# One eigensolver on one Trainium2 core: a factor formed on other engines, levels interleaved, fewer waits inside an engine

## The chip, the core and the metric

The program runs on one core of a Trainium2 chip. Its time is the time of one execution on the device in microseconds (us), given as the median of several runs. Engines are named as in the profile: PE is TensorE, DVE is VectorE, ACT is ScalarE, POOL is GpSimd, SP is SyncE. Everything is float32.

## The reference, cut to what matters

Input `x` is (128 batches, 128 nodes, 128 features) and `adj` is a 128x128 symmetric matrix. Two layers follow each other:

```
deg = sum(A, 0) + sum(A, 1) - diag(A)
L   = rsqrt(deg)[:, None] * (diag(deg) - A) * rsqrt(deg)[None, :]
_, U = eigh(L)                                   # 128 eigenvectors
h = relu(layernorm(x))
x = x + einsum('nm,bmd->bnd', U, relu(einsum('mn,bnd->bmd', U.T, h) @ W1 + b1) @ W2 + b2)
h = relu(layernorm(x))
x = x + conv_and_LSTM(h)        # two graph convolutions, then windows of 1 to 4 nodes through LSTM cells
```

The signs of the eigenvectors must be those that the reference's solver gives, because a ReLU stands between `U.T` and `U`.

## The kernel before, in words

The first half of the time is the eigensolver, and it is a serial chain. Engines run their own instruction streams and wait for each other on semaphores. Nothing is scheduled automatically: the order in each stream is the order in which the code stands. In order of time DVE does this:

1. **Householder**, 127 steps that make the matrix tridiagonal (DVE, PE and ACT in turn). After 16 steps POOL gets a 16x16 corner and starts 16 sweeps of its own (the `leaf` tiles, `Fori` at L307): they settle the sign of the leaf and end with `leaf_sign` (L378).
2. **Statistics and the orthogonal factor** (L906 to L956). Layer norm statistics of `x`, then `QT` from the Householder vectors: six rounds in which DVE copies two PE results out of PSUM and PE multiplies them again, and two more products. DVE waits for PE in each.
3. **First Sturm count** (`sturm`, L974 to L999): 127 steps on 128x16 tiles from both ends of the matrix, then one comparison over 128x2048 and one sum over it. Then 16 comparisons, each multiplied with ones by PE and summed in PSUM (L1004, L584). **Second Sturm count** likewise, without the products.
4. **Setting up four levels** (L1019 to L1033): `D4`, `EV`, `lam4` and `wrow` hold the matrix cut in 1, 2, 4 and 8 blocks.
5. **Two twisted passes** (`twisted`, L1039 to L1088): 127 recurrence steps of 8 lanes, then for each of the four levels, one after the other, a chain of 128x128 instructions that ends in a vector `V4[:, l]`.
6. **Tail** (L1092 to L1158): normalizing, the deflation and sign rules, `QT` times the vectors, two refinements in which DVE and PE alternate, the last signs, and `eig_done`.

In DVE's stream two helpers do the waiting. `op` (L742) waits for the instruction that it has just issued before the next one may start. `ask` (L746) issues one, tells PE, and then waits for PE's answer. POOL has an `op` of the same kind (L311), so each of its 88 instructions in a sweep waits for the one before.

While DVE runs the second Sturm count and the first twisted pass, PE and ACT transpose and multiply the normalized `x` for the first layer (`turn`, `first_product`). PE's stream is in order: the `QT` products, the transposes of the LSTM weights (L570 to L581), the 16 count products (L584), then this work. After `eig_done` the first layer's products start (L629), then the LSTM rounds follow; nothing of that part depends on how the eigensolver was done.

Of the kernel before, what the change touches and what calls it, by code (L numbers as in the profile page):

```python
# [11 lines left out]
F = 16  # L12
# [47 lines left out]
def build(nc, t_in, out):  # L60
    with ExitStack() as ctx:
# [21 lines left out]
        scp = sb("scp", [N, 64])  # L83
# [98 lines left out]
        stv = sem("stv")  # L182
        stored = sem("stored")
# [40 lines left out]
        ring = [spare[:, (8 + c) * GW:(9 + c) * GW] for c in range(RING)]  # L224

# [46 lines left out]
        def _(pool):  # L272
# [34 lines left out]
            with nc.gpsimd.Fori(0, QR_SWEEPS) as k:  # L307
# [20 lines left out]
                for c, v in enumerate((d16[:, 1:16], d16[:, 0:15], e16[:, 0:15])):  # L328
                    op(TT(pick[:, c, 0:15], v, oh[:, 0:15], ALU.mult))
# [29 lines left out]
                for w in (1, 2, 4, 8):  # L359
                    op(TT(lift[:, w:LEAF], now[:, w:LEAF], y16[:, 0:LEAF - w], ALU.mult))  # L360
# [23 lines left out]
        def _(act):  # L384
# [17 lines left out]
            nc.scalar.activation(ln[:, 2, :], ln[:, 1, :], ACT.Sqrt).then_inc(ln_dev, 1)  # L402
            for c in range(2 * SKIPS):
                act.wait_ge(w_turned, c + 1)
                nc.scalar.activation(wT[:, c // SKIPS, c % SKIPS, :], banks[c % 2][:], ACT.Copy).then_inc(w_kept, 1)
# [114 lines left out]
        def _(pe):  # L520
# [34 lines left out]
            mms((B[3], M[1]), (B[4], Um))  # L555
            mms((B[3], M[1], M[0]), (B[4], M[0], M[1]))
            for r in range(6):
                if r < 5:
                    mms((B[5], M[4], M[6]), (B[3], M[4], M[3]), (B[4], M[3], M[4]))
                else:  # L560
                    mms((B[5], M[4], M[6]))
            mms((B[3], M[7], M[8]))
            mms((B[3], M[8], M[5]))
# [18 lines left out]
            for f in range(F):  # L582
                pe.wait_ge(stv, f + 1)
                ins = nc.tensor.matmul(banks[6][:, 0:1], BIG[:, f * N:(f + 1) * N], ones[:, 0:1],  # L584
                                       start=(f == 0), stop=(f == F - 1))
# [28 lines left out]
            mms((B[3], V4[:, 0, :]), (banks[6][:, 0:1], sc[:, 30:31].to_broadcast([N, N]), ones[:, 0:1]))  # L614
            mms((B[3], M[1], QT[:]), (B[4], QT[:], M[1]), (banks[5][:, 0:1], QT[:], sc[:, 31:32]))
            for r in range(REFINES):
                mms((B[3], Lap[:], U[:]))
                mms((B[4], U[:], M[0]), (B[5], U[:], U[:]))
                mms((B[6], ones[:], M[5]))
                mms((B[3], UT[:], M[5]), (B[4], M[5], UT[:]))  # L620
            mms((banks[3][:, 0:1], U[:], sc[:, 32:33]))
            mms((B[4], UT[:]))

            pe.wait_ge(eig_done, 1)
            for it in range(ROUNDS):
# [6 lines left out]
                for i in range(STREAMS):  # L632
# [6 lines left out]
                    last.then_inc(out_ready[i], 1)  # L639
                for i in range(STREAMS):  # L640
                    pe.wait_ge(out_kept[i], it + 1)
                    nc.tensor.matmul(bank[i][(3 * it + 2) % 2], UT[:], z0S[i], start=True, stop=True).then_inc(back_ready[i], 1)
# [94 lines left out]
        def _(dve):  # L737
# [27 lines left out]
            op(V.memset(UC[:], 0.0))  # L765
            dve.wait_ge(adj_in, 16)
# [139 lines left out]
            op(V.tensor_scalar(hB[:], hB[:], -1.0, None, ALU.mult))  # L906
# [30 lines left out]
            ask(V.tensor_tensor(M[2], A[:], I, ALU.mult))  # L937
            op(V.tensor_copy(dB[:], B[3]))
            op(V.tensor_tensor(M[1], B[4], below[:, 0:N], ALU.mult))
            ask(V.tensor_tensor(M[1], M[1], hB[:], ALU.mult))  # L940
            op(V.tensor_copy(M[0], B[3]))
            op(V.tensor_copy(M[8], B[4]))
            dve.wait_ge(ln_var, 1)
            dve.wait_ge(ln_dev, 1)
            V.tensor_tensor(M[6], I, M[0], ALU.add).then_inc(to_pe, 1)
            inverse(slice(0, BATCH))
            answered[0] += 1
            asked[0] += 1
            dve.wait_ge(from_pe, answered[0])
            for r in range(6):  # L950
# [8 lines left out]
            LO, HI, H1, H2, LAM = 18, 19, 33, 34, 35  # L959
            op(V.scalar_tensor_tensor(out=M[0], in0=eB[:], scalar=-1.0, in1=eB[:], op0=ALU.mult, op1=ALU.max))  # L960
            op(V.tensor_copy(M[1], M[0]))
            op(V.tensor_tensor(M[1][:, 1:N], M[1][:, 1:N], M[0][:, 0:N - 1], ALU.add))
            op(V.tensor_tensor(M[3], dB[:], M[1], ALU.subtract))
            op(V.tensor_reduce(S(LO), M[3], AX_X, ALU.min))
            op(V.tensor_tensor(M[3], dB[:], M[1], ALU.add))
            op(V.tensor_reduce(S(HI), M[3], AX_X, ALU.max))
            op(V.tensor_scalar(S(H1), S(HI), S(LO), 1.001 / (N * F), ALU.subtract, ALU.mult))
            op(V.scalar_tensor_tensor(out=S(LO), in0=S(H1), scalar=-0.5, in1=S(LO), op0=ALU.mult, op1=ALU.add))
            op(V.tensor_tensor(M[2], eB[:], eB[:], ALU.mult))
            op(V.tensor_scalar(M[2], M[2], TINY, -1.0, ALU.max, ALU.mult))  # L970
# [3 lines left out]
            def sturm(sem):  # L974
# [43 lines left out]
            for l in range(LEVELS):  # L1018
                op(V.tensor_copy(D4[:, l, :], dB[:] if l == 0 else D4[:, l - 1, :]))  # L1019
                op(V.tensor_copy(EV[:, l, :], eB[:] if l == 0 else EV[:, l - 1, :]))  # L1020
                op(V.tensor_copy(lam4[:, l:l + 1], S(LAM)))
                for c in (SPLITS[l - 1] if l else []):
                    op(V.tensor_scalar(D4[:, l, c - 1:c + 1], D4[:, l, c - 1:c + 1], M[0][:, c - 1:c], None,
                                       ALU.subtract))
                    op(V.memset(EV[:, l, c - 1:c], 0.0))
            op(V.memset(wrow[:], 0.0))
            for l in range(3):
                for c in SPLITS[l]:

                    op(V.memset(wrow[:, l, c - 1:c], 1.0))  # L1030
# [64 lines left out]
            for l in range(LEVELS):  # L1095
                op(V.tensor_scalar(V4[:, l, :], V4[:, l, :], S(24 + l), None, ALU.mult))
# [202 lines left out]
```

## Time and profile before

| | us |
|---|---|
| median of 3 runs | 1615.69 (1614.9 to 1615.76) |
| the profiled execution, its own time | 1614.43 |
| its span in the trace | 1612.7 |
| DVE busy | 1164.6 (72%) |
| PE busy | 1207.6 (75%) |
| POOL busy | 508.7 (32%), all before 700 us but for one instruction |

The profile shares the chain of work that ended last as PE 55%, DVE 39%, issue 3%, ACT 3%. The span of the trace and the time of the execution differ by 1.73 us, which lie around the program. A busy share is an average over two halves: in the first DVE carries the chain, in the second PE. Starts in the timeline rows are counted from the start of the span, and two rows of one engine overlap where the second did not wait for the first.

### The profile page before, as it was taken

How to read it: one execution, taken by the hardware profiler on the slowest of the kernel's cores; microseconds unless marked ns; L12 is line 12 of the kernel's file. 1: busy time of each engine (PE TensorE's matmuls, PEld its weight loads, DVE VectorE, ACT ScalarE, POOL GpSimd, SP SyncE). 2: the span in 40 equal slices, each digit the busy share in tenths (PEclk: the TensorE clock that was granted, in tenths of full speed). 3: DMA queues.
4: the chain of work that ended last, by engine and by line, in shares of the span. 5: the costliest groups of instructions: out<-in, count | busy, mean ns of one | idle time of the engine just before them, and what ended most of it. 6: DMA issues, size and time to landing. Idle time of an engine off the chain costs nothing.

```text
span 1612.7 us, 26217 instructions
## 1 busy us (share of the span) xinstructions
PE 1207.6 (75%) x7124; PEld 1077.3 (67%) x7124; DVE 1164.6 (72%) x6182; ACT 790.9 (49%) x2549; POOL 508.7 (32%) x1426
## 2 busy tenths in 40 slices
PE   5666777775436500016989999999999999999998
PEld 4555666665335400005868989989898998989897
DVE  8999999998689999975775654645555564555545
ACT  1222222221219700001237868688786868868676
POOL 0277777777887778720000000000000000000000
PEclk9999999999859955556999999999999999999999
DMA  9200000000000000000310000000000000000000
GB/s 269 58 1 1 1 1 1 1 1 1 1 0 1 1 0 0 1 1 26 101 32 1 2 26 0 26 0 13 13 0 26 0 26 0 0 26 0 26 1 27
DMA packets 43626, 28.77 MB, mean 18 GB/s; under 512 B 1520, under 2 KB 39440, under 8 KB 43536
## 3 DMA queue, kind: packets, MB, share of 16 engines
q1 hardware_dynamic: 43536, 27.81, 6.1%
q8 instruction: 27, 0.44, 0.1%
q14 instruction: 63, 0.52, 0.1%
HBM read 19.42 MB, written 8.39 MB: 17 GB/s over the span
## 4 chain that ended last, share of the span: by engine, by line
PE 55%; DVE 39%; issue 3%; ACT 3%; DMA 0%; ACTq 0%; DVEq 0%
PE bank L705 12%; PE bank L695 9%; PE bank L700 7%; PE bank L708 7%; PE bank L543 5%; DVE PV L1058 4%; DVE RC L1052 3%; DVE PV L994 2%; DVE wB L847 2%; PE bank L629 2%; PE bank L637 2%; PE bank L669 2%; PE bank L677 2%; PE bank L663 2%; DVE sc L857 2%
## 5 line engine op out<-in xcount | busy, mean ns | idle before, releaser
L705 PE MATMUL bank<-spare,wT 128*128 128x256 f32 (+2 forms) x1408 | 311.2, 321 | 0.0
L474 ACT ACTIVATE PV<-bank,bias 128x256 f32<-128x256 f32 (+2 forms) x704 | 305.2, 437 | 0.0
L474 ACT ACTIVATE BIG<-bank,bias 128x128 f32<-128x128 f32 (+2 forms) x544 | 228.2, 420 | 117.3 <-PE bank L708 101.2
L705 PEld LDWEIGHTS bank<-spare,wT 128*128 128x128 f32 x1408 | 234.8, 191 | 13.2
L695 PE MATMUL bank<-spare,wT 128*128 128x128 f32 (+2 forms) x1088 | 228.2, 320 | 4.3 <-DVE spare L1218 2.9
L1204 DVE TENSOR_TENSOR BIG<-BIG,PV 128x128 f32<-128x128 f32 (+2 forms) x192 | 62.9, 328 | 209.8 <-ACT BIG L474 209.7
L695 PEld LDWEIGHTS bank<-spare,wT 128*128 128x128 f32 x1088 | 168.7, 190 | 22.9 <-DVE spare L1218 9.5
L708 PE MATMUL bank<-spare,wT 128*128 128x128 f32 (+2 forms) x768 | 169.7, 303 | 0.0
L392 ACT ACTIVATE sc<-bank 128x1 f32<-128x1 f32 x127 | 21.7, 171 | 261.9 <-PE bank L538 261.9
L700 PE MATMUL bank<-spare,wT 128*128 128x128 f32 (+2 forms) x768 | 141.5, 307 | 3.6 <-DVE spare L1216 1.2
L538 PE MATMUL bank<-ident 128*128 128x2 f32 x254 | 74.4, 363 | 92.1 <-DVE ident L863 91.0
L354 POOL TENSOR_TENSOR leaf<-leaf 128x1 f32<-128x1 f32 x240 | 134.6, 561 | 20.0
L482 ACT ACTIVATE spare<-spare 128x256 f32<-128x256 f32 (+2 forms) x352 | 134.7, 383 | 6.9 <-DVE spare L1207 6.9
L538 PEld LDWEIGHTS bank<-ident 128*128 128x128 f32 x254 | 63.7, 311 | 103.1 <-DVE ident L863 101.7
L1201 DVE TENSOR_TENSOR spare<-BIG,PV 128x256 f32<-128x256 f32 (+2 forms) x160 | 60.8, 380 | 97.5 <-ACT PV L474 97.5
L708 PEld LDWEIGHTS bank<-spare,wT 128*128 128x128 f32 x768 | 125.2, 191 | 3.3
L700 PEld LDWEIGHTS bank<-spare,wT 128*128 128x128 f32 x768 | 113.8, 191 | 13.8 <-DVE spare L1216 10.5
L528 PE MATMUL bank<-ident,V 128*128 128x128 f32 x1 | 0.4, 447 | 157.1 <-DVE sc L1101 157.1
L528 PEld LDWEIGHTS bank<-ident,V 128*128 128x128 f32 x1 | 0.2, 182 | 157.3 <-issue 157.3
L543 PE MATMUL bank<-A,UC 128*128 128x127 f32 (+63 forms) x254 | 87.5, 442 | 15.5 <-DVE UC L827 4.5
L352 POOL TENSOR_SCALAR leaf<-leaf 128x1 f32<-128x1 f32 x240 | 89.9, 375 | 25.1
L1058 DVE SCALAR_TENSOR_TENSOR PV<-RC,m,PV 128x4 f32<-128x4 f32 x508 | 90.7, 220 | 0.0
(355 smaller groups left out, 2850.6 us busy)
## 6 DMA issues: line engine op xcount, KB each, us to landing
spare<-in_x SPq DMA_DIRECT2D x32, 256.0 KB, 3.6
out<-X SPq DMA_DIRECT2D x32, 256.0 KB, 2.4
spare<-in_L_gnn_Wih SPq DMA_DIRECT2D x4, 256.0 KB, 4.2
spare<-in_L_gnn_Whh SPq DMA_DIRECT2D x4, 256.0 KB, 4.1
W<-in_L_gnn_W SPq DMA_DIRECT2D x2, 64.0 KB, 2.5
Wg<-in_L_gnn_Wg SPq DMA_DIRECT2D x2, 64.0 KB, 2.3
adj<-in_adj SPq DMA_DIRECT2D x1, 64.0 KB, 1.8
X<-in_x SPq DMA_DIRECT2D x4, 0.5 KB, 17.3
```

Source lines behind the costliest of these rows:

```text
L352: op(TS(am[:, i + 1:i + 2], rho[:, i:i + 1], ne16[:, i:i + 1], am[:, i + 1:i + 2], ALU.mult, ALU.add))
L354: op(TT(rho[:, i + 1:i + 2], am[:, i + 1:i + 2], neg16[:, 0:1], ALU.pow))
L474: last = nc.scalar.activation(gate_out[q][i][:, 0:T], gate(i, q, T), ACT.Tanh if q == GATE_G else ACT.Sigmoid, bias=bias[:, at:at + 1])
L482: nc.scalar.activation(tS[i][:, 0:T], cS[i][:, 0:T], ACT.Tanh).then_inc(tanh_ready[i], 1)
L538: nc.tensor.matmul(banks[7][:, 0:2], x_wide, ident[:, t:N + 1:N - t], start=True, stop=True).then_inc(s_ready, 1)
L543: nc.tensor.matmul(banks[1][:, live(k)], u_c.to_broadcast([N, N]), A[:, live(k)], start=True, stop=True).then_inc(pb_ready, 1)
L695: last = nc.tensor.matmul(gate(i, q, T), wT[:, 0, p - 1, q * D:(q + 1) * D], xt, start=True, stop=(j == 0))
L700: last = nc.tensor.matmul(gate(i, q, T), wT[:, 1, p - 1, q * D:(q + 1) * D], hS[i][:, 0:T], start=False, stop=True)
L705: last = nc.tensor.matmul(gate(i, q, T), wT[:, 0, p - 1, q * D:(q + 1) * D], xt, start=True, stop=(j == 0))
L708: last = nc.tensor.matmul(gate(i, q, T), wT[:, 1, p - 1, q * D:(q + 1) * D], hS[i][:, 0:T], start=False, stop=True)
L1058: s.did(V.scalar_tensor_tensor(out=nx, in0=RC[:, last + lane:last + lane + live], scalar=M[2][:, row:row + 1], in1=nx, op0=ALU.mult, op1=A ...
L1204: V.tensor_tensor(gI[i][:, 0:T], gI[i][:, 0:T], gG[i][:, 0:T], ALU.mult).then_inc(cell_part[i], 1)
```

## The change

Helpers are added: `go` issues a DVE or POOL instruction without waiting, and a wait for its number is put ahead of its first reader. `tell` and `hear` split `ask` in two, so that other instructions can stand between them. `also` counts a second answer from PE.

- **The factor.** The six rounds, `QT` and its last two products leave DVE's stream. DVE writes one start matrix (`Q1`) and goes on; PE and ACT form powers and sums in `ahead` and banks 3 to 6 by themselves and leave `QT`.
- **Set-up.** `D4`, `EV` and `wrow` are filled before the first Sturm count, with fewer and wider instructions; only `lam4` is left after the second.
- **Counts.** The comparison over 128x2048 and the sum over it become comparisons and additions on quarters and a sum over 128x512. Of the 16 comparisons after the first count, 14 add up on DVE, and PE does 2 products in place of 16.
- **Twisted passes.** The chains of the four levels are issued side by side, two levels in one 128x256 instruction where that can be. The last four small operations serve all levels at once.
- **Tail.** The vectors of levels 1 to 3 aren't normalized; their sums are scaled instead. The refinement takes column sums by PE in place of a diagonal, and the sign rules stand where DVE would wait for PE. `leaf_sign` is waited for only behind the second refinement's step. The last signs are applied to `U` and `UT` by row and column, without the last transpose. `eig_done` counts to 2: PE waits for 1 ahead of L629's products and for 2 ahead of the first products with `UT`.
- **POOL.** The sweep keeps 88 instructions; 14 start without any wait, and 11 more wait only for one further back than the last.

```diff
+            def go(ins):
+                return t.did(ins)
+            def tell(ins):
+                ins.then_inc(to_pe, 1)
+                asked[0] += 1
+                answered[0] += 1
+                return answered[0]
+            def hear(answer):
+                dve.wait_ge(from_pe, answer)
...
+            rows = tell(V.tensor_tensor(M[2], A[:], I, ALU.mult))
+            op(V.scalar_tensor_tensor(out=QH, in0=hB[:], scalar=-1.0, in1=below[:, 0:N], op0=ALU.mult, op1=ALU.mult))
             for b in range(STEPS - BN_LAG, BATCH):
                 x_statistics(b)
+            hear(rows)
+            go(V.tensor_copy(dB[:], B[3]))
+            V.tensor_tensor(Q1, B[4], QH, ALU.mult).then_inc(q_in, 1)
...
-            for r in range(6):
-                op(V.tensor_copy(M[3], B[3]))
-                ask(V.tensor_copy(M[4], B[4]))
-                op(V.tensor_tensor(M[6], M[6], B[5], ALU.add))
-            ask(V.tensor_tensor(M[7], M[6], hB[:], ALU.mult))
-            ask(V.tensor_copy(M[5], B[3]))
-            op(V.tensor_tensor(QT[:], I, B[3], ALU.add))
...
-                op(V.tensor_scalar(pivots, pivots, 0.0, None, ALU.is_lt))
-                op(V.tensor_reduce(cnt[:], pivots.rearrange("p (i f) -> p f i", f=F), AX_X, ALU.add))
+                n_p = [go(V.tensor_scalar(part[c], part[c], 0.0, None, ALU.is_lt)) for c in range(2)]
+                for c in range(2):
+                    dve.wait_ge(v_, n_p[c])
+                    n_p[c] = go(V.scalar_tensor_tensor(out=part[c], in0=part[2 + c], scalar=0.0, in1=part[c],
+                                                       op0=ALU.is_lt, op1=ALU.add))
+                dve.wait_ge(v_, n_p[1])
+                op(V.tensor_tensor(part[0], part[0], part[1], ALU.add))
+                op(V.tensor_reduce(cnt[:], part[0].rearrange("p (i f) -> p f i", f=F), AX_X, ALU.add))
...
             for r in range(REFINES):
-                if r:
-                    ask(V.tensor_tensor(U[:], U[:], B[3], ALU.add))
-                ask(V.tensor_copy(M[0], B[3]))
+                if r == 0:
+                    lapped = tell(V.tensor_copy(U[:], B[4]))
+                else:
+                    hear(stepped)
+                    lapped = tell(V.tensor_tensor(U[:], U[:], B[3], ALU.add))
+                gram = also()
+                squared = tell(V.tensor_tensor(V4[:, 1, :], U[:], U[:], ALU.mult))
...
+                else:
+                    hear(signs)
+                    n_a = go(V.tensor_copy(M[9], banks[0][:, 0:N]))
+                    dve.wait_ge(leaf_sign, 1)
+                    go(V.scalar_tensor_tensor(out=S(SIGN), in0=S(LFB), scalar=sg[:, 0:1], in1=S(LFA),
+                                              op0=ALU.mult, op1=ALU.add))
...
-                    op(TT(y16[:, w:LEAF], y16[:, w:LEAF], lift[:, w:LEAF], ALU.add))
-                    if w < 8:
-                        op(TT(then[:, w:LEAF], now[:, w:LEAF], now[:, 0:LEAF - w], ALU.mult))
-                        now, then = then, now
+                    if w < 8:
+                        go(TT(then[:, w:LEAF], now[:, w:LEAF], now[:, 0:LEAF - w], ALU.mult))
+                        now, then = then, now
+                    pool.wait_ge(pool_q, n_lift)
+                    op(TT(y16[:, w:LEAF], y16[:, w:LEAF], lift[:, w:LEAF], ALU.add))
```

How instructions stand in a row shows best at three places. On DVE between the Householder steps and the first Sturm count, before, one round of the factor reads:

```order
L951 COPY m<-bank 128x128 [waits v_]
L952 COPY m<-bank 128x128 [waits v_]
L953 TENSOR_TENSOR m<-m,bank 128x128 [waits from_pe]
L951 COPY m<-bank 128x128 [waits v_]
L952 COPY m<-bank 128x128 [waits v_]
L953 TENSOR_TENSOR m<-m,bank 128x128 [waits from_pe]
```

At the same place there now stand the start matrix (L1021; its output in `ahead` is `Q1`) and the statistics:

```order
L1015 TENSOR_TENSOR m<-A,ident 128x128 [waits a_ready,e_ready]
L1016 SCALAR_TENSOR_TENSOR ahead<-hB,below 128x128
L891 BN_STATS stats<-X 128x6 [waits v_]
L891 BN_STATS stats<-X 128x6 x16
L1020 COPY dB<-bank 128x128 [waits from_pe]
L1021 TENSOR_TENSOR ahead<-bank,ahead 128x128
L1028 TENSOR_TENSOR ln<-stats 128x128 [waits bn_done]
```

One wait for PE is left there, and it has the 17 statistics of `x` ahead of it. The second place is DVE behind the recurrence of a twisted pass, before, where one level's chain (`ISA` is the multiply that also sums, with the read of its sum behind it) reads:

```order
L1067 SCALAR_TENSOR_TENSOR m<-PV,lam 128x128 [waits v_]
L1069 TENSOR_TENSOR m<-m,D 128x128 [waits v_]
L1070 SCALAR_TENSOR_TENSOR m<-m 128x128 [waits v_]
L1071 TENSOR_REDUCE sc<-m 128x1 [waits v_]
L1072 TENSOR_SCALAR m<-m,sc 128x128 [waits v_]
L757 ISA m,sc<-m 128x128 [waits v_]
```

After the change the same work of all four levels reads:

```order
L1194 SCALAR_TENSOR_TENSOR BIG<-PV,lam 128x128 x4
L1197 TENSOR_SCALAR RC<-RC 128x1024 [waits v_]
L1198 MEMSET BIG 128x4
L1201 TENSOR_TENSOR BIG<-BIG,D 128x256 [waits v_] x2
L1204 SCALAR_TENSOR_TENSOR BIG<-BIG 128x256 [waits v_] x2
L1208 TENSOR_TENSOR BIG<-EV,RC 128x2x127 [waits v_]
L1208 TENSOR_TENSOR BIG<-EV,RC 128x2x127
L1211 TENSOR_REDUCE sc<-BIG 128x2 [waits v_] x2
```

Each wait that is left names an instruction at least one further back. The third place is POOL at the end of a sweep, now:

```order
L396 TENSOR_TENSOR leaf<-leaf 128x16 [waits pool_q]
L397 TENSOR_TENSOR leaf<-leaf 128x15
L399 TENSOR_TENSOR leaf<-leaf 128x16 [waits pool_q]
L400 TENSOR_TENSOR leaf<-leaf 128x15
L402 TENSOR_TENSOR leaf<-leaf 128x16 [waits pool_q]
L404 TENSOR_TENSOR leaf<-leaf 128x15 [waits pool_q]
L406 TENSOR_TENSOR leaf<-leaf 128x15 [waits pool_q]
L407 TENSOR_TENSOR leaf<-leaf 128x1
```

In the kernel before (L369 to L376) each of these eight waited for the one ahead of it.

## Rows read from the trace of the kernel before

**Rows 1.** Stretches (us): length, busy time (instructions) by engine, granted clock, DMA share.

```profile
core 0: us, PE busy (x) PEld busy (x) DVE busy (x) ACT busy (x) POOL busy (x), PEclk, DMA share, GB/s
710.17:747.69 37.52, 11.23 (x37) 8.36 (x37) 22.34 (x94) 0.20 (x1) 0.00 (x0) 0.50 0.00 0
747.69:1612.70 865.01, 843.17 (x5568) 763.24 (x5568) 481.45 (x1432) 613.03 (x1835) 2.97 (x1) 0.99 0.06 17
```

**Rows 2.** Timeline, DVE, 391 to 426 us: start, duration, instruction, idle and releaser.

```profile
391.38 0.23 DVE L906 TENSOR_SCALAR hB<-hB 128x128 f32<-128x128 f32 x1
391.65 3.39 DVE L807 BATCH_NORM_STATS2 stats<-X 128x6 f32<-128x128 f32 x17
...
401.16 0.29 DVE L945 TENSOR_TENSOR m<-ident,m 128x128 f32<-128x128 f32 x1
401.37 0.94 DVE L927 RECIPROCAL ln<-ln 128x128 f32<-128x128 f32 x1
...
425.29 2.29 DVE L975 TENSOR_TENSOR PV<-dB,XG 128x2048 f32<-128x2048 f32 x1
```

**Rows 3.** Timeline, DVE, end of the first Sturm count.

```profile
464.88 1.29 DVE L998 TENSOR_SCALAR PV<-PV 128x2048 f32<-128x2048 f32 x1
466.21 3.57 DVE L999 TENSOR_REDUCE cnt<-PV 128x16 f32<-128x2048 f32 x1
469.81 3.29 DVE L1004 TENSOR_SCALAR BIG<-iota_f,cnt 128x128 f32<-128x128 f32 x16
477.21 0.22 DVE L1007 TENSOR_SCALAR sc<-bank,sc 128x1 f32<-128x1 f32 x1 [4.11 <-PE bank L584]
```

**Rows 4.** Timeline, DVE, setting up the levels and the start of the recurrence.

```profile
523.72 0.23 DVE L1019 COPY D<-dB 128x128 f32<-128x128 f32 x1
...
535.28 0.34 DVE L1041 TENSOR_SCALAR PV<-D,lam 128x128 f32<-128x128 f32 x1
...
538.32 0.24 DVE L1052 RECIPROCAL RC<-PV 128x4 f32<-128x4 f32 x2
```

**Rows 5.** L1061, which ends both recurrences; then timeline, DVE, behind the first.

```profile
L1061 DVE RECIPROCAL RC<-PV x2: 203/203/203, 600.2 to 689.3; 128x8 f32<-128x8 f32 x2
...
603.79 0.42 DVE L1077 TENSOR_TENSOR_SCAN m<-m 128x128 f32<-128x128 f32 x1
...
624.37 0.37 DVE L1041 TENSOR_SCALAR PV<-D,lam 128x128 f32<-128x128 f32 x1
```

**Rows 6.** Timeline, DVE, the tail.

```profile
710.17 0.15 DVE L1092 COPY sc<-sc 128x1 f32<-128x1 f32 x1
...
721.78 0.29 DVE L1124 COPY U<-bank 128x128 f32<-128x128 f32 x1
722.96 0.29 DVE L1128 COPY m<-bank 128x128 f32<-128x128 f32 x1 [0.89 <-PE bank L530]
...
744.13 0.29 DVE L1148 TENSOR_TENSOR U<-U,bank 128x128 f32<-128x128 f32 x1
```

**Rows 7.** Timeline, PE: count products, first layer's first and second products with U.

```profile
470.19 6.98 PE L584 MATMUL bank<-ones,BIG 128*128 128x1 f32 x32 [40.44 <-DVE BIG L1004]
...
747.69 5.74 PE L629 MATMUL bank<-U,X 128*128 128x128 f32 x32 [0.38 <-DVE U L1158]
...
760.27 3.73 PE L629 MATMUL bank<-U,X 128*128 128x128 f32 x32
```

**Rows 8.** Timeline, POOL: two at the start, one sweep instruction, the last of the leaf.

```profile
1.58 0.24 POOL L280 IOTA iota_f<- 128x128 f32 x1
1.79 0.14 POOL L282 IOTA iota_p<- 128x1 f32 x1
...
478.08 2.45 POOL L352 TENSOR_SCALAR leaf<-leaf 128x1 f32<-128x1 f32 x1
...
697.24 0.19 POOL L378 COPY leaf<-leaf 128x1 f32<-128x1 f32 x1 [0.23 <-POOL leaf L376]
```

**Rows 9.** Groups by line, POOL: busy, mean ns of one, idle before.

```profile
L352 POOL TENSOR_SCALAR leaf<-leaf 128x1 f32<-128x1 f32 x240 | 89.9, 375 | 25.1
L354 POOL TENSOR_TENSOR leaf<-leaf 128x1 f32<-128x1 f32 x240 | 134.6, 561 | 20.0
```

More of the change, by code:

```diff
@@ L581, in _ @@
             nc.tensor.matmul(banks[1][:, 0:N], bg0B[:], adjT[:], start=True, stop=True).then_inc(small_turned, 1)
[L582 to L585, printed above, removed]
+            for c in range(2):
+                pe.wait_ge(stv, c + 1)
+                ins = nc.tensor.matmul(banks[6][:, 0:1], BIG[:, c * N:(c + 1) * N], ones[:, 0:1],
+                                       start=(c == 0), stop=(c == 1))
             ins.then_inc(from_pe, 1)
@@ L765, in _ @@
             op(V.memset(UC[:], 0.0))
+            op(V.memset(wrow[:], 0.0))
             dve.wait_ge(adj_in, 16)
@@ L936, in _ @@
             variance(slice(0, BATCH))
[L937 to L942, printed above, removed]
+            LO, HI, H1, H2, LAM = 18, 19, 33, 34, 35
+            n_e = go(V.scalar_tensor_tensor(out=M[0], in0=eB[:], scalar=-1.0, in1=eB[:], op0=ALU.mult, op1=ALU.max))
@@ L943, in _ @@
+            t.last(dve)
+            op(V.tensor_scalar(XG[:], grid[:], S(H1), S(LO), ALU.mult, ALU.add))
             dve.wait_ge(ln_var, 1)
             dve.wait_ge(ln_dev, 1)
[L945 removed]
             inverse(slice(0, BATCH))
[L947 to L950, printed above, removed]
[L951 to L953 removed]
@@ new lines, in twisted @@
+                for l in range(LEVELS):
+                    if not vectors:
+                        go(V.tensor_tensor_reduce(out=GAM[:, l, :], in0=GAM[:, l, :], in1=ONE[:, l, :], scale=1.0,
+                                                  scalar=0.0, op0=ALU.mult, op1=ALU.add, accum_out=S(GSUM + l)))
+                for h in TWO:
+                    dve.wait_ge(v_, n_zu[h.stop - 1])
+                    n_zd[h.start] = go(V.tensor_tensor(ZD[:, h, :], ZD[:, h, :], ZU[:, h, :], ALU.add))
+                for h in TWO:
+                    dve.wait_ge(v_, n_zd[h.start])
+                    n_v[h.start] = go(V.tensor_tensor(V4[:, h, :], ZD[:, h, :], ONE[:, h, :], ALU.subtract))
@@ new lines, in twisted @@
+                for l in range(LEVELS):
+                    dve.wait_ge(v_, n_v[l // 2 * 2])
+                    go(V.tensor_tensor_reduce(out=ZD[:, l, :], in0=V4[:, l, :], in1=V4[:, l, :], scale=1.0, scalar=0.0,
+                                              op0=ALU.mult, op1=ALU.add, accum_out=S(NORM + l)))
+                t.last(dve)
+                if not vectors:
+                    op(V.reciprocal(S(RQ, LEVELS), S(NORM, LEVELS)))
+                    op(V.tensor_tensor(S(RQ, LEVELS), S(RQ, LEVELS), S(GSUM, LEVELS), ALU.mult))
+                    op(V.tensor_scalar(S(RQ, LEVELS), S(RQ, LEVELS), RAYLEIGH_CLIP, -RAYLEIGH_CLIP, ALU.min, ALU.max))
+                    op(V.tensor_tensor(lam4[:], lam4[:], S(RQ, LEVELS), ALU.add))
@@ new lines, in _ @@
+            largest = tell(V.tensor_tensor(S(30), lam4[:, 0:1], ident[:, N - 1:N], ALU.mult))
+            CC, ZZ, LF, SIGN, LFA, LFB = 44, 47, 50, 54, 55, 40
+            for l in range(LEVELS - 1):
+                go(V.scalar_tensor_tensor(out=GAM[:, l, :], in0=V4[:, l + 1, :], scalar=-1.0, in1=V4[:, l + 1, :],
+                                          op0=ALU.mult, op1=ALU.max))
+            dve.wait_ge(rs_out, 2)
+            op(V.reciprocal(S(INV, LEVELS), S(INV, LEVELS)))
+            turned = tell(V.tensor_scalar(V4[:, 0, :], V4[:, 0, :], S(INV), None, ALU.mult))
@@ new lines, in _ @@
+            hear(largest)
+            op(V.tensor_scalar(S(43), banks[6][:, 0:1], DEFLATE, None, ALU.mult))
+            t.last(dve)
+            hear(turned)
+            dve.wait_ge(v_, n_31)
+            first = tell(V.tensor_copy(M[1], B[3]))
+            second = also()
+            for l in range(LEVELS - 1):
+                go(V.tensor_tensor_reduce(out=ONE[:, l, :], in0=V4[:, 0, :], in1=wrow[:, l, :], scale=1.0, scalar=0.0,
+                                          op0=ALU.mult, op1=ALU.add, accum_out=S(CC + l)))
+                go(V.tensor_tensor_reduce(out=GAM[:, l, :], in0=GAM[:, l, :], in1=wrow[:, 3 + l, :], scale=1.0, scalar=0.0,
+                                          op0=ALU.mult, op1=ALU.add, accum_out=S(ZZ + l)))
@@ new lines, in _ @@
+            hear(stepped)
+            by_row = tell(V.tensor_tensor(U[:], U[:], B[3], ALU.add))
+            by_col = also()
+            told()
+            n_u = go(V.tensor_tensor(M[0], U[:], M[9], ALU.mult))
+            hear(second)
+            op(V.tensor_tensor(UT[:], UT[:], B[2], ALU.add))
+            n_w = go(V.tensor_scalar(M[1], UT[:], S(SIGN), None, ALU.mult))
+            hear(by_row)
+            n_r = go(V.tensor_tensor(M[2], B[6], M[9], ALU.mult))
+            hear(by_col)
+            n_c = go(V.tensor_tensor(S(53), banks[5][:, 0:1], S(SIGN), ALU.mult))
```

439 lines of the change are left out of this document (286 added, 153 removed).

## The prediction

> **What bounds the kernel now.** I read the table of stretches first, then DVE's timeline, then the ends of PE's and POOL's work. From the first products with `U` at 747.69 us to the end there are 865.01 us in which PE is busy 843.17 at a granted clock of 0.99 [rows 1]. The change leaves nearly nothing different there, so I take this part to move as a block. Everything ahead of 747.69 is a chain that DVE carries, with PE's answers in it. What matters is how often DVE waits for its own last instruction or for PE. Two 128x128 instructions start 0.21 us apart when the second does not wait for the first, though each takes 0.29: 401.16 and 401.37, and 17 statistics in 3.39, 0.20 each [rows 2]. Where each waits for the one before, the distance is the duration and some 0.03 more: 0.32. So an edge taken out between independent instructions is worth about 0.12. A question to PE costs 1.18 from the start of one DVE instruction to the start of the next, 0.89 of it idle [rows 6]. POOL is a second chain: its leaf ends at 697.24 [rows 8], and today DVE asks for it only some 20 us later.
>
> Widths: (2.29 - 0.29) us over 1920 more columns is 1.04 ns a column [rows 2], so 256 columns take 0.42 and start 0.335 apart, 512 take 0.69. A comparison with constants takes 1.29 for 2048 [rows 3], by 0.15 fixed about 0.43 for 512.
>
> **The change, part by part**, new times worked out with these distances (0.32 waiting, 0.205 not).
>
> 1. Householder's end to the first Sturm count: 391.38 to 425.29 is 33.9 us [rows 2]. Now: 0.5 for two instructions, 3.4 statistics, 0.4 for `dB` and `Q1`, 2.1 variance as before; set-up: two copies of 512 columns (0.45 each; 0.7 at worst), eight 128-wide ones with 0.205, one with 0.15, small fills, cuts and rows of `wrow` 2.3, one wait 0.1, `XG` 0.33, `inverse` 2.4 as before. Sum 13.8: **20.1 saved**. PE's and ACT's new chain starts near 396. PE had 40.44 us idle ahead of the count products [rows 7]; seven rounds at the old round's 2.7 (DVE's two copies become ACT's) and four more steps end near 420, where the old one ended, and the transposes of weights follow. The products now come 21 us earlier, so some 19 of the 40 are left: cost nothing. If the chain took twice as long, PE would be late by about 1 us.
> 2. End of each Sturm count: 464.88 to 469.81 is 4.93 [rows 3]. Now 0.34 + 0.34 + 0.60 + 0.72 + 0.72 and a sum over 512 columns at the old 1.67 ns (1.0): 3.8. Twice 1.15: **2.3 saved**.
> 3. The products: 469.81 to 477.21 is 7.4, of which 4.11 idle, PE taking 6.98 for 16 [rows 3, 7], 0.44 each. Now 16 DVE instructions in 3.3 and two products, the last ending 0.85 later: 4.2. **3.2 saved**.
> 4. Set-up between 523.72 and 535.28, 11.56 [rows 4]; one copy of 0.19 is left. **11.4 saved** (its new place is paid in 1).
> 5. Eight subtractions ahead of each recurrence, 3.04 [rows 4]: written with a stride, 0.34 each, 0.255 apart now, 2.16. Twice: **1.8 saved**. The recurrences (62 us each) aren't touched.
> 6. Behind the first recurrence 600.2 to 624.37, 24.2 [rows 5]. Now: four strided ones 1.6, the limit over 1024 columns 0.6, ten 256-wide ones (differences, absolute values, least, sums, vectors) at 0.335, 3.4; four strided 256-wide products 2.2; four comparisons 0.8; eight scans, 0.42 long [rows 5], 0.335 apart, 2.7; eight multiply-and-sum 2.4; wait and four small ones 0.9. Sum 14.6: **9.6 saved**. The scans are the dearest unknown: waiting each, they cost 0.9 more.
> 7. Behind the second, 689.3 to 710.17, 20.9 [rows 5, 6], by the same list without four sums and the small ones 12.6: **8.3 saved**.
> 8. Tail, 710.17 to 747.69, 37.5 [rows 6, 7]. First part to `U`, 11.6 before: root, reciprocal and one scaling 1.3, transpose 0.85 (an estimate; 1.18 at most, as a product), six sums behind `M[1]` 2.0 (PE's 1.18 lies under them): 4.0. The two refinements, 22.35 before. Each now has one way to `M[5]`: 1.18 for the first product, two reciprocals of 0.94, some 14 further 128-wide ones, of which half wait; PE's five products (0.44 each behind one another, as in [rows 7]) end at 2.9, under the first reciprocal. That is 6.0, and 6.3 in the second, which also writes two diagonals. Behind the first `M[5]` stand 2.1 us of sign rules where PE's answer needs 1.18, behind the second 0.9 under 1.18. So 8.3 and 7.4. The end, 3.56 before: 1.4 for the two small products, 0.7 to `U`: 2.15. Sum 21.9: **15.6 saved**.
> 9. A fill of `wrow` (768 columns) ahead of the wait for `adj`: 0.2 lost.
>
> 20.1 + 2.3 + 3.2 + 11.4 + 1.8 + 9.6 + 8.3 + 15.6 - 0.2 = 72.1. PE starts on `U` at 675.6. `UT` comes 0.5 later, under 32 products.
>
> **The leaf.** DVE waits for it at about 672.6, and from its end to PE's start there are 2.7 us, so the leaf is free of cost if it ends before 673. It ends at 697.4 now. In a sweep 25 instructions no longer wait for the one before. L354 idles 20.0 us over 240 [rows 9]: 0.08 an edge; and the starts of the two that don't wait lie 0.21 apart at a duration of 0.24 [rows 8], another 0.03 to 0.06. At 0.08, 25 x 16 edges give 32 us and an end at 665; at 0.14, 56 and 641. I take 0.14. It has to be 0.061 at least.
>
> Against it: one 1-column instruction of the sweep took 2.45 us where the mean of its group is 0.375 [rows 8, 9]; it started at 478.08, where DVE begins the second count with a 128x2048 subtraction of two operands in SBUF; that of the first count took 2.29 [rows 2]. So a wide DVE instruction holds POOL up until it ends. The change sets wide instructions closer, in some 30 us behind the recurrences and ahead of the first count. If there each of about 38 POOL instructions waited out a 0.42, that is 16 us: 657 from the middle, 681 from the poor end.
>
> The Trainium skill, "SBUF — State Buffer", section "Who interferes with whom", says that a DVE instruction with two inputs in SBUF and a GpSimd one that reads SBUF exclude each other, and that the second fully blocks until the first is done. The row of 2.45 us agrees. By this rule alone, without room between DVE's instructions, POOL would stand still for all of those 30 us.
>
> **Sum.** The profiled execution is 1614.43 (span 1612.7 and 1.73 around it): 1614.43 - 72.1 = 1542.3. The median shown is 1.26 above it: 1543.6, and I forecast 1544.
>
> **The rivals.**
> - A: the leaf becomes the bound. At the poor end of both (681) PE starts at 683.7 and 8 us are lost: 1552. With no gain from the edges it ends at 697.4, PE starts at 700.1, 24.5 lost: 1568. For it: 697.24 lies 24 us behind the forecast's wait. Against: the idle time between POOL's instructions is in the rows, and needs only three quarters of it. 0.11.
> - B: instructions issued without a wait don't close up as reckoned, because of strides, 256-wide operands or POOL's hold on memory. Some 14 edges in 1, 16 in 5, 60 in 6 and 7 and 20 in 8, 110 of them at 0.12: 13 us less, 1557; half of it is 1550 and lies in the forecast's own range. Against: 401.16 and 401.37 were 0.21 apart with POOL at work. 0.07.
> - C, slower: the clock. PE is granted 0.50 in the tail, its lower level of 1.2 GHz [rows 1], after having had nothing to do since the first layer's first products. Its first 32 products with `U` took 5.74, the next 3.73 [rows 7], so the clock rose to 2.4 GHz within the first. If the changed pattern of work ahead let it stay low through the first layer's eight rounds (three such groups each, some 10.6 us a round, 85 us in all), these would cost twice as much: 1544 + 85 - 2 = 1627. It is slower than before from seven low rounds on (72 over 10.6 is 6.8). Against: the tail gets denser, more products in 22 us than now lie in 37.5. 0.02.
> - D: a wait that I haven't seen eats up nearly all. 0.01.
>
> **How the numbers follow.** Forecast 0.79, with its own range 1537 to 1553: below by an earlier rise of the clock (2) and by 5 for my rounding of small instructions, above by half of B and the poor values of scans and copies. The range 1536 to 1562 takes in A at its poor end and B, and leaves out A's far end and C. What a measurement of this kernel can tell from no change is about 0.2%, 3.2 us. Faster by more 0.97, within 0.01, slower 0.02.
>
> **What would show it.** DVE's first 128x2048 subtraction near 405; the first count's next instruction near 453; L1191 (end of the first recurrence) near 562; the root's copy near 654; L378's successor, the last of POOL, near 641 to 665; PE's first product with `U` near 676; 865 us behind it. The forecast fails if DVE sits idle ahead of the instruction that reads the leaf's sign, if distances without a wait are over 0.25, or if PE's chain for `QT` ends behind 445.

## The result, and the profile after

The changed kernel takes 1541.34 us, median of 4 runs (1540.52 to 1543.1), against 1615.72 for the kernel before (also 4 runs): the ratio is 0.9541 (95% interval 0.953 to 0.9552), 74 us less. The forecast was 1544. The profiled execution took 1543.1, the longest of the four; its span is 1541.4.

DVE's timeline of the changed kernel from the end of the Householder steps to the first Sturm count, its rows answering to [rows 2]:

```profile
392.95 0.29 DVE L1015 TENSOR_TENSOR m<-A,ident 128x128 f32<-128x128 f32 x1
393.16 0.36 DVE L1016 SCALAR_TENSOR_TENSOR ahead<-hB,below 128x128 f32<-128x128 f32 x1
...
399.52 0.42 DVE L1050 COPY D<-dB 128x512 f32<-128x512 f32 x1
399.86 0.42 DVE L1051 COPY EV<-eB 128x512 f32<-128x512 f32 x1
...
400.45 0.28 DVE L1055 TENSOR_TENSOR m<-eB 128x128 f32<-128x128 f32 x1
400.65 0.28 DVE L1057 TENSOR_TENSOR m<-dB,m 128x128 f32<-128x128 f32 x1
...
403.47 0.95 DVE L1038 RECIPROCAL ln<-ln 128x128 f32<-128x128 f32 x1 [0.17 <-DVE XG L1091]
...
405.91 2.29 DVE L1099 TENSOR_TENSOR PV<-dB,XG 128x2048 f32<-128x2048 f32 x1
```

12.96 us stand where 33.91 stood, and the set-up of the levels is in them. L1055 and L1057 start 0.20 apart and last 0.28. The one wait for PE that is left, ahead of L1020, costs no idle time. The count's end and the setting-up behind the second count, answering to [rows 3, 4]:

```profile
445.72 0.76 DVE L1123 TENSOR_SCALAR PV<-PV 128x512 f32<-128x512 f32 x2
446.40 1.29 DVE L1126 SCALAR_TENSOR_TENSOR PV<-PV 128x512 f32<-128x512 f32 x2
447.72 0.69 DVE L1129 TENSOR_TENSOR PV<-PV 128x512 f32<-128x512 f32 x1
448.45 1.00 DVE L1130 TENSOR_REDUCE cnt<-PV 128x16 f32<-128x512 f32 x1
449.49 0.48 DVE L1134 TENSOR_SCALAR BIG<-iota_f,cnt 128x128 f32<-128x128 f32 x2
449.89 3.75 DVE L1138 SCALAR_TENSOR_TENSOR BIG<-iota_f,cnt,BIG 128x128 f32<-128x128 f32 x14
454.49 0.22 DVE L1145 TENSOR_SCALAR sc<-bank,sc 128x1 f32<-128x1 f32 x1 [0.84 <-PE bank L651]
...
500.05 0.17 DVE L1156 COPY lam<-sc 128x4 f32<-128x4 f32 x1
500.25 0.34 DVE L1170 TENSOR_SCALAR PV<-D,lam 128x128 f32<-128x128 f32 x1
```

The 14 adding comparisons take 3.75 us and start 0.26 apart, not 0.205. They last longer too, 0.34 each. The wait for the sum that stood two instructions ahead is not what spaces them. The same stretch in narrower windows:

```profile
449.70 0.28 DVE L1134 TENSOR_SCALAR BIG<-iota_f,cnt 128x128 f32<-128x128 f32 x1
449.89 0.60 DVE L1138 SCALAR_TENSOR_TENSOR BIG<-iota_f,cnt,BIG 128x128 f32<-128x128 f32 x2
```

The second adding comparison reads what this L1134 left at 449.98, and yet it starts only at 450.16. Behind the first recurrence and then in the tail, answering to [rows 5, 6]:

```profile
563.81 0.20 DVE L1191 RECIPROCAL RC<-PV 128x8 f32<-128x8 f32 x1
563.93 1.47 DVE L1194 SCALAR_TENSOR_TENSOR BIG<-PV,lam 128x128 f32<-128x128 f32 x4
...
567.26 1.16 DVE L1208 TENSOR_TENSOR BIG<-EV,RC 128x254 f32<-128x254 f32 x2
...
570.85 0.42 DVE L1219 TENSOR_TENSOR_SCAN BIG<-BIG 128x128 f32<-128x128 f32 x1
571.19 0.40 DVE L1220 TENSOR_TENSOR_SCAN BIG<-BIG 128x128 f32<-128x128 f32 x1
...
577.45 0.34 DVE L1170 TENSOR_SCALAR PV<-D,lam 128x128 f32<-128x128 f32 x1
...
652.93 0.15 DVE L1245 COPY sc<-sc 128x1 f32<-128x1 f32 x1
...
656.60 0.28 DVE L1273 COPY U<-bank 128x128 f32<-128x128 f32 x1
...
665.43 0.29 DVE L1276 TENSOR_TENSOR U<-U,bank 128x128 f32<-128x128 f32 x1
...
671.90 0.21 DVE L1339 SCALAR_TENSOR_TENSOR sc<-sc,leaf 128x1 f32<-128x1 f32 x1
...
672.74 0.29 DVE L1345 TENSOR_TENSOR U<-U,bank 128x128 f32<-128x128 f32 x1 [0.37 <-PE bank L584]
```

L1339 is the first to read the leaf's sign, and it has no idle time ahead of it. POOL's last instruction for the leaf, in the view of its line (least, median and longest in ns, then the time), which answers to [rows 8]:

```profile
L409 POOL COPY leaf<-leaf x1: 183/183/183, 654.7 to 654.7; 128x1 f32<-128x1 f32 x1
```

PE's timeline of the changed kernel at its first products with `U`, which answers to [rows 7]:

```profile
674.85 6.79 PE L710 MATMUL bank<-U,X 128*128 128x128 f32 x32 [0.75 <-DVE U L1361]
...
688.49 3.73 PE L710 MATMUL bank<-U,X 128*128 128x128 f32 x32
```

The leaf ended 17 us ahead of its reader. Term by term, with the forecast of each:

| | before | after | saved | forecast |
|---|---|---|---|---|
| up to the end of Householder | 391.38 | 392.95 | -1.6 | -0.2 |
| 1. to the first count | 33.91 | 12.96 | 20.9 | 20.1 |
| 2. ends of both counts | 9.87 | 7.61 | 2.3 | 2.3 |
| 3. count products | 7.40 | 5.00 | 2.4 | 3.2 |
| 4. set-up behind the counts | 11.56 | 0.20 | 11.4 | 11.4 |
| 5. subtractions (with the recurrences) | 129.77 | 127.07 | 2.7 | 1.8 |
| the counts' recurrences | 79.28 | 79.64 | -0.4 | 0 |
| 6. behind the first recurrence | 24.2 | 13.6 | 10.6 | 9.6 |
| 7. behind the second | 20.9 | 12.0 | 8.9 | 8.3 |
| 8. tail | 37.52 | 21.92 | 15.6 | 15.6 |
| PE starts on U | 747.69 | 674.85 | 72.8 | 72.1 |
| from there to the end | 865.01 | 866.55 | -1.5 | 0 |

### The profile page after: what moved, and what is told of

It reads as the page before. It is cut to its first block, busy times and chain, and to the rows that moved or that the text cites. A ratio compares the mean times of both kernels' runs of the same rounds, so it can differ in the third digit from the quotient of the medians.

```text
span 1541.4 us, 26140 instructions
## 1 busy us (share of the span) xinstructions
PE 1202.5 (78%) x7121; PEld 1074.2 (70%) x7121; DVE 1130.8 (73%) x6077; ACT 795.0 (52%) x2572; POOL 495.6 (32%) x1426
## 4 chain that ended last, share of the span: by engine, by line
PE 56%; DVE 38%; issue 3%; ACT 3%; ACTq 0%; DVEq 0%
PE bank L788 13%; PE bank L778 9%; PE bank L783 7%; PE bank L791 7%; PE bank L597 6%; DVE PV L1188 5%; DVE RC L1182 4%; DVE PV L1118 2%; DVE wB L931 2%; PE bank L710 2%; PE bank L718 2%; PE bank L752 2%; PE bank L760 2%; PE bank L746 2%; DVE sc L941 2%
## 5 line engine op out<-in xcount | busy, mean ns | idle before, releaser
L380 POOL TENSOR_TENSOR leaf<-leaf 128x1 f32<-128x1 f32 x240 | 134.4, 560 | 20.0
L783 PEld LDWEIGHTS bank<-spare,wT 128*128 128x128 f32 x768 | 113.8, 191 | 13.8 <-DVE spare L1422 10.5
L378 POOL TENSOR_SCALAR leaf<-leaf 128x1 f32<-128x1 f32 x240 | 93.8, 391 | 23.4
L597 PEld LDWEIGHTS bank<-A,UC 128*128 128x128 f32 x254 | 63.6, 311 | 39.3 <-DVE UC L911 39.3
```

The lines of the kernel that those rows point to most:

```text
L378: op(TS(am[:, i + 1:i + 2], rho[:, i:i + 1], ne16[:, i:i + 1], am[:, i + 1:i + 2], ALU.mult, ALU.add))
L380: op(TT(rho[:, i + 1:i + 2], am[:, i + 1:i + 2], neg16[:, 0:1], ALU.pow))
L597: nc.tensor.matmul(banks[1][:, live(k)], u_c.to_broadcast([N, N]), A[:, live(k)], start=True, stop=True).then_inc(pb_ready, 1)
L783: last = nc.tensor.matmul(gate(i, q, T), wT[:, 1, p - 1, q * D:(q + 1) * D], hS[i][:, 0:T], start=False, stop=True)
```

## The experiments

Each ran on one chip together with others of its batch and with the kernel before. In the first batch (e1 to e4) that took 1614.31 us, in the second (e5 to e8) 1615.46. The changed kernel's own 1541.34 is from a third, with 1615.72, so differences between batches are uncertain by some 1.4 us: set against the kernel before of its own batch, e1, e3 and e4 lie 30.3, 26.3 and 20.5 us above the change, not 28.9, 24.9 and 19.1.

**e1: POOL's sweep put back.**

```diff
-                go(TT(y16[:, 0:15], d16[:, 0:15], d16[:, 1:16], ALU.mult))
...
+                op(TT(tmp[:, 0:15], d16[:, 0:15], d16[:, 1:16], ALU.mult))
...                      # all 88 instructions as in the kernel before
```

> The changed kernel with POOL's sweep put back: each of the 88 instructions waits for the one before. Theory (the leaf's chain has slack only because of the shorter sweep): it ends at about 697, as before, DVE stands at the instruction that reads its sign from 671.9 on, PE starts on U 2.7 us after the leaf's end, at 700: 25 us later than 674.85, so 1566 us. Rival (the leaf has slack anyway, or the last instruction could be overtaken): 1541 to 1543. Second question: the Householder part ended 1.6 us later in the changed kernel than before; if POOL's denser stream slows DVE there, 1.2 us of it vanish here.

It took 1570.23 us, ratio 0.9729 (0.9713 to 0.9745), 4 us more than expected. Who DVE waited for from 391 to 705 us, the longest first (us in total, times, longest):

```profile
DVE sc L1329 <- POOL leaf L399: 30.7, 1, 30.7
DVE sc L1135 <- PE bank L641: 0.8, 1, 0.8
```

And DVE at the leaf's reader, then POOL's last instruction, then PE on `U`:

```profile
700.96 0.22 DVE L1329 SCALAR_TENSOR_TENSOR sc<-sc,leaf 128x1 f32<-128x1 f32 x1 [30.68 <-POOL leaf L399]
```

```profile
700.74 0.19 POOL L399 COPY leaf<-leaf 128x1 f32<-128x1 f32 x1 [0.23 <-POOL leaf L397]
```

```profile
703.58 5.62 PE L700 MATMUL bank<-U,X 128*128 128x128 f32 x32 [0.75 <-DVE U L1351]
```

So without the shorter sweep 29 of the 74 us are lost. From the leaf's end (700.93) to PE's start there are 2.65 us, the 2.7 of the prediction. The leaf ended 3.5 us later than in the kernel before with the same sweep. The Householder part ended at 391.6 (L1006 at 391.79, one instruction behind it), 1.4 us sooner than in the first trace of the changed kernel. Between traces of kernels with the same stream there (the changed kernel and e3 to e8) this point lies anywhere from 392.15 to 392.97, so the 1.4 is good to some 0.8 us.

**e2: the new sweep alone, in the kernel before.** The same edit the other way round.

> The kernel before with the new POOL sweep alone. Theory: the leaf isn't on the chain there, so the time stays within 0.2% of 1615.7, perhaps 1 us longer if POOL's denser stream costs DVE something in the Householder steps; the leaf ends at about 655 instead of 697. Rival (the shorter sweep itself gives part of the 74 us, by leaving memory to DVE behind its end): 1600 to 1610.

1615.31 us, ratio 1.0005 (0.9996 to 1.0015): no change, as the theory has it. The end of the leaf, and DVE's first row behind the Householder part (391.38 before):

```profile
649.26 0.18 POOL L388 COPY leaf<-leaf 128x1 f32<-128x1 f32 x1 [0.23 <-POOL leaf L386]
```

```profile
392.20 0.24 DVE L916 TENSOR_SCALAR hB<-hB 128x128 f32<-128x128 f32 x1
```

48.0 us less over 25 x 16 edges are 0.12 an edge; the leaf ended 6 us sooner than the 655 that I expected. The shorter sweep is worth nothing by itself, and 29 us beside the rest. It seems to cost DVE some 0.8 us in the Householder steps; that is one trace against one.

**e3: DVE's `go` waits again.**

```diff
             def go(ins):
-                return t.did(ins)
+                n = t.did(ins)
+                t.last(dve)
+                return n
```

> The changed kernel in which DVE's go waits again for its own instruction, in the same order and with the same widths; POOL and the questions to PE stay. It measures what leaving out waits is worth by itself. Theory (about 0.12 us for each of some 110 edges): 13 us more, 1554. Rival 1 (the gain is in the wider instructions and fewer questions to PE alone): within 3 us of 1541. Rival 2 (an edge is worth more than 0.12, because waits also hold instructions that PE waits for): over 1560.

1566.22 us, ratio 0.9701 (0.9685 to 0.9717): 25 us more than the changed kernel, twice what I expected. PE started on `U` at 699.08, 24.2 us later. The same four and two instructions as above, waiting:

```profile
572.34 1.95 DVE L1196 SCALAR_TENSOR_TENSOR BIG<-PV,lam 128x128 f32<-128x128 f32 x4
...
577.02 1.29 DVE L1210 TENSOR_TENSOR BIG<-EV,RC 128x254 f32<-128x254 f32 x2
...
581.88 0.42 DVE L1221 TENSOR_TENSOR_SCAN BIG<-BIG 128x128 f32<-128x128 f32 x1
582.34 0.42 DVE L1222 TENSOR_TENSOR_SCAN BIG<-BIG 128x128 f32<-128x128 f32 x1
```

1.95 for 1.47, and scans 0.46 apart instead of 0.32 to 0.34. The program issues 196 instructions through `go` on DVE, so one of them is worth 24.2 / 196 = 0.12 us in the mean; behind a few (the second L1126, for one) the changed kernel waits anyway. The value of a wait was right; I had counted 110 of them. Rival 2's bound (over 1560) was passed, but not for its reason. Of the 74 us about a third is left-out waits alone. By subtraction, the rest is in wider and fewer instructions and in questions to PE; no run separates these two.

**e4: the four levels in turn.**

```diff
-                n_r = go(V.reciprocal(RC[:, (N - 1) * LANES:], PV[:, (N - 1) * LANES:N * LANES]))
...                      # side by side
                 for l in range(LEVELS):
...
+                    op(V.scalar_tensor_tensor(out=M[3], in0=qb, scalar=lam4[:, l:l + 1], in1=qf,
+                                              op0=ALU.add, op1=ALU.add))
...                      # as before, each waiting
```

> The changed kernel with the four levels behind each recurrence in turn again, as before (128-wide, each waiting). Theory (the two terms of 10.6 and 9.0 us are on the chain in full): 19.6 us more, 1561. The leaf then ends 35 us ahead of its reader, which costs nothing. Rival (part of the gain only moves DVE to a later wait): under 1555.

1560.42 us, ratio 0.9668 (0.9652 to 0.9684), 19.1 more than 1541.34 and 20 more than e8: the two terms are on the chain in full.

**e5: DVE waits for the factor.**

```diff
             op(V.tensor_scalar(XG[:], grid[:], S(H1), S(LO), ALU.mult, ALU.add))
+            dve.wait_ge(q_act, sum_kept(DOUBLINGS) + 2)
             dve.wait_ge(ln_var, 1)
```

> The changed kernel with one wait added: DVE waits, ahead of the layer norm's last step before the first Sturm count, until PE and ACT have left QT. It takes the cover away from the factor. In the changed kernel QT's last copy ends at 413.36 us and DVE reaches this point at 403.4. Theory (the factor costs nothing only because DVE doesn't wait for it): 10.0 us more, 1551. Rival (PE and ACT finish sooner when DVE keeps still, or the wait is cheap): under 1548.

It took 1550.47 us, ratio 0.9601 (0.9586 to 0.9616), 10.0 more than e8. DVE's row behind the wait, and ACT's last copy:

```profile
412.59 0.95 DVE L1038 RECIPROCAL ln<-ln 128x128 f32<-128x128 f32 x1 [10.07 <-ACT QT L456]
```

```profile
412.22 0.28 ACT L456 ACTIVATE QT<-bank 128x128 f32<-128x128 f32 x1 [0.80 <-PE bank L630]
```

The chain isn't cheap, it is covered. PE reached its count products with room: its last work ahead of them ended at 420.6 in the changed kernel, and it sat idle for 32.9 us until the first of them at 453.44. QT's chain ended at 413.4 there, 32 us ahead of the 445 that would have been too late.

**e6 and e7: idle products for PE's clock.** e7 has both parts, e6 only the first.

```diff
+            def fill(count):
+                for _ in range(count):
+                    nc.tensor.matmul(banks[7][:, 3 * N:4 * N], ident[:, 0:N], ident[:, 0:N], start=True, stop=True)
+            pe.wait_ge(tw2, 460)
+            fill(66)
             mms((banks[6][:, 0:1], sc[:, 30:31].to_broadcast([N, N]), ones[:, 0:1]))
...
                     mms((banks[0][:, 0:2 * N], ones[:], diag2))
+                fill(7 if r else 14)        # e7 alone, and others like it
```

> The changed kernel with 66 idle products on PE (128x128, into an unused part of bank 7, read by nobody), started at the 460th step of the second recurrence, so that they run from about 635 us on and end ahead of the tail. PE stood at a granted 0.50 in the tail and took 6.79 us for its first 32 products with U, where 3.73 is what they take at full clock. Theory (the clock follows PE's recent work, and the tail's own work doesn't keep it high): the first questions of the tail get cheaper, the clock falls again in its gaps, and the time is 0 to 2 us less than 1541. Rival 1 (once high, the clock stays through the tail): 5 to 7 us less, 1535. Rival 2 (the products end too late and PE's first answer is late): over 1543.

> As the one before, and 38 more idle products in the tail where PE waits for DVE (1, 14, 7, 7 and 2 and again 7 behind the refinements' steps). Theory (these keep the clock high): questions to PE in the tail cost about 0.3 us less each, ten of them, and the first products with U take 3.7 in place of 6.8: 5 to 6 us less than 1541, 1535. Rival (the clock stays low or the idle products stand ahead of DVE's questions): 1541 to 1547.

> The changed kernel itself, for comparison with these on the same chip: 1541, with the first 32 products with U between 5.4 and 6.8 us long (5.74 before, 6.79 after, 5.4 to 6.6 in the four experiments so far).

e8, the changed kernel again: 1540.46 us (1540.04 to 1542.06). e6: 1540.24 (1540.11 to 1542.22), ratio to before 0.9537 (0.9524 to 0.955): no change. e7: 1538.71 (1537.21 to 1539.61), ratio 0.9527 (0.9514 to 0.954). In stretches, first e6 (length, then busy time and instructions of PE, PEld, DVE, ACT, POOL, the granted clock, DMA):

```profile
635.00:640.00 5.00, 5.00 (x30) 5.00 (x30) 5.00 (x42) 0.00 (x0) 4.13 (x10) 0.61 0.02 3
640.00:650.00 10.00, 10.00 (x92) 10.00 (x91) 9.97 (x31) 0.00 (x0) 9.06 (x11) 1.00 0.00 1
650.00:660.00 10.00, 5.42 (x33) 4.60 (x31) 9.04 (x50) 0.21 (x1) 8.82 (x21) 0.80 0.01 2
660.00:665.00 5.00, 1.62 (x6) 1.33 (x7) 4.61 (x21) 0.00 (x0) 2.83 (x10) 0.50 0.00 0
```

Then e7:

```profile
660.00:665.00 5.00, 3.62 (x29) 3.20 (x28) 4.49 (x20) 0.00 (x0) 1.52 (x9) 1.00 0.00 0
665.00:672.00 7.00, 5.09 (x34) 4.10 (x32) 6.77 (x28) 0.00 (x0) 0.00 (x0) 1.00 0.00 0
```

And e8:

```profile
660.00:665.00 5.00, 1.29 (x5) 0.99 (x5) 4.61 (x22) 0.00 (x0) 2.65 (x10) 0.50 0.00 0
665.00:672.00 7.00, 4.66 (x16) 3.57 (x16) 6.10 (x24) 0.00 (x0) 0.00 (x0) 0.50 0.00 0
```

In e6 the clock rises to 2.4 GHz ahead of the tail and is down at 1.2 again from 660 on, by PE's own sparse work. In e7 it stays up. Its idle products in the tail were 31 (1, 14, 7, 7 and 2), fewer than the 38 that the expectation names. The gain of 1.7 us over e8 is smaller than the 5 to 6 that I expected. Both halves of the sum fell short. The tail took 20.7 us (from 651.75 to PE's start on `U` at 672.49) against 21.9 in e8 (652.11 to 674.01), 1.2 less and not 3: DVE bounds most of it, being busy for 19.3 of its 22 us in the changed kernel. The first 32 products took 3.84 against 5.33, 1.5 less and not 3: in e8 they were shorter than the 5.4 to 6.8 that I had given for it. The ranges of e7 and e8 don't touch, but the intervals of their ratios to the kernel before overlap, so e7 is the shortest version that was run, and I don't call its lead over the changed kernel settled.

## Why the prediction was right

**What bounds the kernel** held: the second half moved as a block (865.01 and 866.55), and the whole gain lies ahead of PE's first product with `U`.

**Terms 1, 2, 4, 6, 7 and 8** came within 1 us each. The rule behind them, 0.32 us for a 128x128 instruction that waits and 0.205 for one that doesn't, is in the rows above, and 1.04 ns for each more column holds where two tensors are read (L1129: 0.69 for 512). The two copies of 512 columns don't follow it: they took 0.42 and started 0.34 apart, less than both of my prices. The scans closed up (0.32 to 0.34), so their dear end was not needed. Terms 2, 4, 5 and 8 have no run of their own; they are read from the rows of one trace.

Two of the sums don't come out as written. The parts listed in term 1 add up to 14.2 us, not 13.8, and the stretch took 12.96, because the set-up took 3.7 (399.32 to 403.01) where its parts were given 5.0. In term 8 the parts of the way to `M[5]` add up to 6.7, not 6.0, since I let half of the 14 wait; fewer did, and the way took 6.0 (656.92 to 662.90). With the parts as listed the forecast would have been some 2 us longer.

**Term 3** was too high by 0.8. I took 0.205 for all 16 comparisons; an adding one lasts 0.34 and starts 0.26 behind the last. With every wait put back (e3) the 14 take 5.27, 0.38 apart, so leaving the wait out is worth 0.12 here too: what I had wrong was the instruction's own length. By these rows a third chain side by side would gain nothing; no run tried it.

**Term 5** was too low by 0.9: the strided subtractions start 0.20 apart, not 0.255.

**Term 9**, the start, was mis-sized: 0.2 forecast, 1.6 measured. The fill of `wrow` ahead of the wait for `adj` cost 0.3. The rest grew over the Householder steps. With the old sweep in the same kernel (e1) this part ended at 391.6, with the new sweep in the kernel before (e2) at 392.2, with both between 392.2 and 393.0 in seven traces. With the 0.3 of the fill taken off, all eight traces with the new sweep end later than both with the old, by 0.4 to 1.4 us. That is what the new sweep's denser stream seems to cost DVE there. POOL did 805 instructions between 66 and 392 us where it had done 742. That is the far side of the hold that I had weighed only for POOL's delay.

**The leaf** was the step on which most hung, and it held with room: needed were 0.061 us an edge, I took 0.14, and e2 shows 0.12. Its end was forecast between 641 and 665 and came at 654.7, at 662.8 in e8. e1 shows what rival A is worth: 29 us, 4.4 more than its far end, because the leaf ends 3.5 us later even with the old sweep and DVE has become faster ahead of it.

**The hold of wide DVE instructions on POOL** was there, and was small in time. POOL in e8 behind the second recurrence (start, duration):

```profile
641.28 1.55 POOL L378 TENSOR_SCALAR leaf<-leaf 128x1 f32<-128x1 f32 x1
642.91 0.61 POOL L380 TENSOR_TENSOR leaf<-leaf 128x1 f32<-128x1 f32 x1
643.62 1.29 POOL L378 TENSOR_SCALAR leaf<-leaf 128x1 f32<-128x1 f32 x1
645.00 0.55 POOL L380 TENSOR_TENSOR leaf<-leaf 128x1 f32<-128x1 f32 x1
645.65 1.05 POOL L378 TENSOR_SCALAR leaf<-leaf 128x1 f32<-128x1 f32 x1
```

The same instruction takes 0.375 in the mean of the kernel before (L352 in [rows 9]); here it waits out one wide DVE instruction or several. In the three kernels with the new sweep whose DVE still waits in this place (e2, e3, e4) the leaf ended at 649.3, 650.5 and 650.9; in those without waits (the changed kernel, e5 to e8) between 654.7 and 663.0. So the hold costs POOL 4 to 14 us, somewhat under my 16, and 7.6 us at the least were left of its room (e6: the leaf's end at 663.14, its reader at 670.72). Its 240 instructions of L378 say the same: 85.4 us in all in e2, 93.8 in the changed kernel, 101.5 in e8. The Trainium skill, "SBUF — State Buffer", section "Who interferes with whom", has the second comer fully blocked until the first has finished. The durations of 1.05 to 1.55 agree with it, and some are longer than any one DVE instruction there. POOL did not stand still for the whole 30 us, though, as the rule alone would have it: it went on at two thirds of its pace. In e8 eight pairs of L378 and L380 took 1.60 us each under DVE's wide instructions (563.71 to 576.51); in e5 such pairs took 1.09 at the same time, with DVE still in its recurrence. The changed kernel's first trace had only three such pairs in that stretch, so how much POOL loses depends on where in its sweep the stretch meets it.

**Rival B** did not happen, and I had mis-stated its price: waiting everywhere would have cost 25 us (e3), not 13.

**Rival C**, the clock. It was 0.50 in the tail, and the first 32 products took 6.79 where they had taken 5.74. This isn't the change's doing: e2, with the old tail, had them at 6.56, e1 and e4, with the new, at 5.62 and 5.41, and e8, the same program again, at 5.33. It makes up 1 of the 1.5 us by which the second half is longer in this trace. The length of the second half goes with it in all ten traces: 863.0 us with 3.84 (e7), 864.5 to 865.0 with 5.2 to 5.7, 865.9 to 866.8 with 6.5 to 6.8.

**How much of the hit is luck.** The mechanism held in each part. That the saved time came out within 1 us of the sum (72.8 for 72.1) is partly luck: terms 1, 5, 6 and 7 gave 0.8, 0.9, 1.0 and 0.6 us more than forecast, and the start, the counts' recurrences and term 3 took 1.4, 0.4 and 0.8 of that back. QT's chain and the room ahead of the count products were off as well, at no cost: 413 for about 420, 33 us for 19.

## What to carry to other kernels

A chain of small instructions on one engine, each waiting for the last, pays about 0.12 us for every wait that stands between independent ones: count the instructions, all of them, and multiply. Interleaving parts whose data don't meet takes that back, if enough of them stand side by side. An instruction that doesn't wait starts some 0.08 to 0.1 us ahead of the last one's end in most of these rows (0.29 long and 0.205 apart, 0.34 and 0.26, 0.44 and 0.36; the strided subtractions, 0.34 and 0.20, are an exception), so a longer one mostly gets back the same 0.12, and no more. When one chain is shortened, look for the other that used to end in its shade: here the leaf's shorter sweep is worth nothing alone and 29 us beside the rest.

## What the runs showed of the hardware

- An engine's independent instructions overlap on POOL too: 0.12 us for each wait taken out of the sweep (48.0 us over 400).
- A denser POOL stream of 1- and 16-column instructions seems to slow DVE's small ones: some 0.4 to 1.4 us over the Householder steps, all eight traces with it against the two without.
- The granted clock went from 0.50 (630 to 635 us in e6) over 0.61 (635 to 640) to 1.00 (640 to 650), with PE busy throughout from 635 on, and back to 0.50 within the tail where PE was busy 5.42 of 10 us and then 1.62 of 5. In e7 with 3.62 of 5 and 5.09 of 7 it stayed at 1.00. A product in the tail then took 0.49 us in place of 0.80, and the whole kernel became only 1.7 us shorter.
- The end of the leaf differs by 8 us between two executions of the same program (654.7 and 662.8) whose times differ by 2.6 us (1543.1 and 1540.46).
